# A decoder layer on one core: stacks of two heads by half of the tokens instead of one head by all of them, and keys as 1024 and chunks of 256

## The chip, the cores and the metric

The kernel runs on one core of a Trainium2 chip. Times are device microseconds (us) of that core, the median of several executions. A profile is one further execution. Its engines are called PE (TensorE), DVE (VectorE), ACT (ScalarE), POOL (GpSimd) and SP (the queue that issues most DMAs).

## What is computed

A post-norm decoder layer over 1024 tokens of width 128: self attention with 16 heads of width 8 that share one key and one value head, cross attention over 6404 context rows with a mask, and a top-1 mixture of 8 experts.

```
x = layernorm(x + attn(x))            # Q: 16 heads of 8; K = x@Wk+bk, V = x@Wv+bv: one head of 8 for all
x = layernorm(x + cross(x, ctx, mask))
    # scores = Q K^T / sqrt(8); where(mask == 0, -1e9, scores); softmax; @ V; @ Wo.T + bo
x = layernorm(x + ffn(x))
    # probs = softmax(x @ router_w.T + router_b); the expert of the largest one;
    # out = (x @ expert_w[e].T + expert_b[e]) * max(probs)
```

The mask of these inputs is the same for every token and leaves the last 1233 of the 6404 keys.

## The kernel before

*Units of work.* Both attentions run through the same pipeline. `Qs` holds, for each of 16 heads, a stack of two products: partitions 0 to 63 carry the queries of the first half of the tokens, partitions 64 to 127 those of the second half (`STACK`, index f). TensorE runs the two as one pair beside each other. Rows (queries on the output partitions, keys along the free dimension) are made only to find each query's maximum: VectorE reduces them (`mxs` L786, `mxc` L937). The maximum is split in two parts, turned by TensorE (`turn_max`, L1289), copied by ScalarE (`max_copy`) and stored by SP into rows of `Qs`, so that the column products (keys on the output partitions) come out with the maximum taken off. ScalarE makes the exponentials of the columns into `prob` (L1102, L1141), TensorE multiplies them by the values into bank O (`add_values`, L1319). `copy_o` takes O away, SP stores it to DRAM (`od`) and brings all heads back at the end (`o_back`).

*Steps.* A step is a column block of 128 keys for both halves, one row unit of a later head and the values of the block before. In self attention a head has 8 steps and 8 row units of 128 x 1024 (L1386 to L1416); rows are 15 units ahead. PSUM: two banks RT of 1024 columns for rows, three banks ST of 512 for columns, one bank O.

*Cross.* Keys are taken in pairs of blocks of PAIR = 640. A head has, for these inputs, n = 2 of them, so 10 steps. Its row units are RU = 6 for each 640 keys: four of 128 x 1024 (512 keys, two halves) and two that hold the last 128 keys of four tiles (128 x 512). `cross` (L1508) writes out the order by hand: `other_blocks`, `next_blocks`, `rows_pairwise`, with the banks of columns in the order BANK (L46). The keys of each head lie in DRAM (`kd`); SP loads them into a ring in `big` (`load_k`, L365) and POOL copies them rounded into `Kr` and `Kc` (`staged`, L544), values into `vst` (L572).

*What lies between the attentions.* After the last self values come: the sums back from DRAM, the reciprocal (L890), its spread over the heads (L1463), the projection (L1475), residual and norm (`statistics` L864, `normalised` L871), the turn of x (L1483), the cross queries (`project_q`), the keys and values of the second pair (L1448), and the loads of `Kl`. POOL counts the mask during self attention (L489 to L506); TensorE sums the counts at steps 117 and 118 (`count_live`), VectorE computes from them where the live keys begin (`steering`, L798), and every engine reads the result into a register.

*The end.* `finish` (L1660) projects, norms, turns x, makes the router logits and the products with all 8 experts (L1671), half of them weighed by VectorE (L995), half by ScalarE (L1180) with POOL's sums (L644).

Of the kernel before, what the change touches and what calls it, by code (L numbers as in the profile page):

```python
# [16 lines left out]
P = 128  # L17
# [7 lines left out]
PAIR = 640  # L25
NBLK = PAIR // P
NP = -(-KEYS // PAIR)
KPAD = NP * PAIR
FRONT = KPAD - KEYS
NB = KPAD // P  # L30

CW = PAIR // 2
CR = KPAD // CW
FLAG_AT = 384
MIN_PAIRS = 2
# [6 lines left out]
RU = 6  # L42
RS = NP + 2
NCOL = 2 * NBLK

BANK = (2, 0, 1, 2, 0, 1, 0, 2, 0, 1)  # L46
AGAIN = tuple(min(d for d in range(1, NCOL) if BANK[k - d] == BANK[k]) for k in range(NCOL))
SELF_U = 8
LA = 7
SLOTS = 5  # L50
HALFT = KPAD // 2
# [5 lines left out]
VW = DH + 1  # L57


def decoder_layer(nc, t, out):  # L60
    ctx = ExitStack()
    with ctx:
# [12 lines left out]

# [5 lines left out]
        bqrow = {a: sb(f"bqrow_{a}", [1, D]) for a in "sx"}  # L84
        bkrow = sb("bkrow", [1, DH])
        bv_x = sb("bv_x", [P, 1])
        krep = sb("krep", [P, 1])
        qrep = {a: sb(f"qrep_{a}", [P, DIRECT]) for a in "sx"}
        kcon = sb("kcon", [P, 1])
        qcon = sb("qcon", [P, DIRECT])  # L90
# [3 lines left out]
        bo = {a: sb(f"bo_{a}", [1, D]) for a in "sx"}  # L94
        wkr, bkr = sb("wkr", [P, 9, DH]), sb("bkr", [1, 9, DH])
        wq0 = {a: sb(f"wq0_{a}", [P, DIRECT, 9, DH]) for a in "sx"}
        bq0 = {a: sb(f"bq0_{a}", [1, DIRECT, 9, DH]) for a in "sx"}
        ident = sb("ident", [P, P])
        sel = sb("sel", [P, 8, HEADS, DH])
        penI = sb("penI", [P, P], BF16)  # L100
        ones = sb("ones", [P, P], BF16)
        onesf = sb("onesf", [P, P])
        orow = sb("orow", [1, P])
        zerof = sb("zerof", [P, (HEADS - DIRECT) * HALF * 4 // P])
# [4 lines left out]
        eps = sb("eps", [P, 1])  # L109
        Qs = sb("Qs", [P, HEADS, HALF], F32R)  # L110
        Kself = sb("Kself", [P, Q], F32R)
        Kc, Kr = sb("Kc", [P, NBLK, P], F32R), sb("Kr", [P, PAIR], F32R)
        vst = sb("vst", [P, NBLK, VW])
# [4 lines left out]
        ctxn = sb("ctxn", [P, 2, PAIR])  # L118
        kx_fa, kx_la, kx_ha = sb("kx_f", [P, PAIR]), sb("kx_lo", [P, PAIR]), sb("kx_hi", [P, PAIR], F32R)
        mxs = sb("mxs", [P, 2, 2, QT])  # L120
        mxc = sb("mxc", [P, 2, 2 * NP, QT])
# [5 lines left out]
        aTr = sb("aTr", [P, Q])  # L127
        den, rden = sb("den", [P, P]), sb("rden", [P, P])
        wcol = sb("wcol", [P, 2 * CR - 1], BF16)
        fl = sb("fl", [CR, 2])  # L130
        sm = sb("sm", [P, 2, NP])
        down = sb("down", [P, NP])
        steer = sb("steer", [1, 4], I32)
# [10 lines left out]


        KL_W, G_W = RS * PAIR, QT * PAIR // 2
        big = sb("big", [P, max(KL_W + 3 * G_W, 2 * HALFT + 3 * HALFT // 4 + KPAD // 2)], I32)
        maskI = [big[:, k * HALFT:(k + 1) * HALFT] for k in range(2)]
        m0 = 2 * HALFT
# [3 lines left out]
        Kl = big[:, 0:KL_W].bitcast(F32).rearrange("p (s k) -> p s k", k=PAIR)  # L153
        Qf = Qs[:, :, :].rearrange("p h q -> p (h q)")
        gint = big[:, KL_W:KL_W + G_W].rearrange("p (t k) -> p t k", k=PAIR)
        grow = big[:, KL_W + G_W:KL_W + 2 * G_W].bitcast(BF16).rearrange("p (t k) -> p t k", k=PAIR)
        gcol = big[:, KL_W + 2 * G_W:KL_W + 3 * G_W].bitcast(BF16).rearrange("p (t k) -> p t k", k=PAIR)
        we = big[:, 0:E * D].bitcast(F32).rearrange("p (e o) -> p e o", e=E)

        vroom = Vx[:, :, :, :].rearrange("p b h w -> p (b h w)")
        xroom = big[:, KL_W:KL_W + 3 * G_W].bitcast(F32)
        qfull = {a: r[:, 0:Q] for a, r in (("s", vroom), ("x", xroom))}
        qlow = {a: r[:, Q:2 * Q] for a, r in (("s", vroom), ("x", xroom))}
# [7 lines left out]
        fx = xT[0:CR, 3 * CW:3 * CW + 2 * CR]  # L173

        e_prod = vroom[:, 0:4 * Q].rearrange("p (t e) -> p t e", e=4 * D)
        e_two = vroom[:, 4 * Q:6 * Q].rearrange("p (t e) -> p t e", e=2 * D)
        e_sum = vroom[:, 6 * Q:7 * Q].rearrange("p (t e) -> p t e", e=D)
        aT, coefT = prob[:, 0, :], prob[0:E, 1, :]

# [1579 lines left out]
```

## Time and profile before

| | us |
|---|---|
| median of 3 runs | 506.13 (505.16 to 506.80) |
| span of the profiled execution | 505.4 |
| PE busy | 482.0 (95%) |
| DVE busy | 419.7 (83%) |
| ACT busy | 368.0 (73%) |
| POOL busy | 209.5 (41%) |

The time of the profiled execution by the clock of the runs isn't listed; its span is 0.7 under their median. Busy time is that in which an instruction of the engine was at work by the profile; for PE the ends are modelled, so that a full PE doesn't say that it couldn't be faster. "Idle before" is the time in which the engine stood before an instruction, with what released it. An engine's shares are means over stages with different limits, so the stages are read one by one. The mean granted clock of TensorE is 0.984 of full speed.

### The profile page before, as it was taken

Reading aid. Unit: us, or ns where it says so; the run is one execution under the profiler, and the core shown is the slowest. Engines: PE = TensorE matmul, PEld = TensorE weight load, DVE = VectorE, ACT = ScalarE, POOL = GpSimd, SP = SyncE. Lnnn points to the kernel's source line nnn. Section 1 sums busy time; section 2 is a strip of 40 time slices with the busy share of each in tenths; the row PEclk is TensorE's granted clock in tenths of the full one; section 3 lists DMA queues with packets and bytes.
Section 4 is the critical chain, followed back from the end, with each engine's and each line's share of the span. In section 5 each row is a group of like instructions: output and inputs, shape, how many; then the busy total and the mean of one; then the engine's idle time right before and its main releaser. Section 6 shows DMA issues by size and latency. Waiting matters only on the chain.

```text
span 505.4 us, 13819 instructions
## 1 busy us (share of the span) xinstructions
PE 482.0 (95%) x4122; PEld 197.3 (39%) x4122; DVE 419.7 (83%) x612; ACT 368.0 (73%) x718; POOL 209.5 (41%) x316
## 2 busy tenths in 40 slices
PE   7999999999999999987999999999999999999983
PEld 2433333333333344632344444444444444433641
DVE  5999999999999926668699989999899899831766
ACT  6358888888888875441678877877878887787263
POOL 4825755885469900132233323333233332320045
PEclk9899999999999999999799999999999999999997
DMA  4859864875453014524133110111111111010101
GB/s 116 350 147 305 280 219 166 298 259 194 167 173 137 12 54 123 161 62 121 42 71 81 41 40 26 40 37 30 38 32 40 40 40 40 27 40 22 43 1 45
DMA packets 21772, 52.58 MB, mean 104 GB/s; under 512 B 5021, under 2 KB 13375, under 8 KB 19649
## 3 DMA queue, kind: packets, MB, share of 16 engines
q1 hardware_dynamic: 18461, 22.46, 16.8%
q0 software_dynamic: 2304, 28.84, 15.4%
q8 instruction: 37, 0.61, 0.5%
q10 hardware_dynamic: 932, 0.37, 0.3%
q14 instruction: 38, 0.31, 0.2%
HBM read 42.10 MB, written 8.94 MB: 101 GB/s over the span
## 4 chain that ended last, share of the span: by engine, by line
PE 81%; DVE 9%; ACT 5%; issue 3%; DMA 1%; SPq 0%; DVEq 0%; POOL 0%; ACTq 0%; POOLq 0%
PE O L1321 32%; PE ST L1555 15%; PE RT L1527 10%; PE ST L1352 10%; PE RT L1338 5%; DVE mxs L786 3%; ACT prob L1102 2%; PE O L1292 1%; DVE mxc L937 1%; PE RT L1231 1%; ACT Vx L1180 1%; PE O L1317 1%; PE RT L1464 1%; ACT prob L1141 1%; PE RT L1679 1%
## 5 line engine op out<-in xcount | busy, mean ns | idle before, releaser
L937 DVE TENSOR_REDUCE mxc<-RT 128x1024 f32 (+1 forms) x192 | 196.1, 1045 | 23.4 <-PE RT L1527 18.9
L1141 ACT ACTIVATE prob<-ST 128x512 f32<-128x512 f32 x320 | 172.4, 596 | 38.7 <-PE ST L1555 36.8
L1102 ACT ACTIVATE prob<-ST 128x512 f32<-128x512 f32 x256 | 138.6, 597 | 24.7 <-PE ST L1352 14.1
L786 DVE TENSOR_REDUCE mxs<-RT 128x2 f32<-128x1024 f32 x128 | 152.7, 1224 | 2.8 <-PE RT L1338 0.6
L1527 PE MATMUL RT<-Kr,Qs 64*128 64x128 f32 (+1 forms) x512 | 121.8, 375 | 2.7 <-DVEq L924 1.2
L1555 PE MATMUL ST<-Qs,Kc 64*128 64x512 f32 x320 | 122.3, 458 | 2.0 <-DMA Qs<-qd_x 1.4
L1321 PE MATMUL O<-prob,vst 128*9 128x256 f32 x1280 | 100.3, 385 | 1.7 <-ACT prob L1141 1.3
L1338 PE MATMUL RT<-Kself,Qs 64*128 64x512 f32 x256 | 89.6, 454 | 1.8 <-DVE Kself L753 0.9
L1352 PE MATMUL ST<-Qs,Kself 64*128 64x512 f32 x256 | 91.2, 450 | 0.0
L1321 PE MATMUL O<-prob,Vs 128*9 128x256 f32 x1024 | 79.3, 381 | 1.5 <-ACT prob L1102 0.7
L1555 PEld LDWEIGHTS ST<-Qs,Kc 64*128 64x128 f32 x320 | 54.5, 187 | 61.2 <-issue 31.6
L1527 PEld LDWEIGHTS RT<-Kr,Qs 64*128 64x128 f32 x512 | 59.0, 186 | 23.8 <-DVE mxc L937 18.4
L572 POOL COPY vst<-Vx 128x27 f32 x64 | 13.1, 205 | 106.4 <-PE O L1321 105.5
L1352 PEld LDWEIGHTS ST<-Qs,Kself 64*128 64x128 f32 x256 | 37.4, 184 | 50.2 <-ACT prob L1102 37.5
L495 POOL TENSOR_SCALAR big<-big 128x3520 uint8<-128x3520 uint32 x16 | 50.0, 3127 | 7.2 <-DMA big<-in_mask 6.8
L547 POOL CAST Kr<-big 128x512 fp32r (+1 forms) x64 | 29.2, 456 | 39.4 <-PE RT L1527 21.1
L1321 PEld LDWEIGHTS O<-prob,vst 128*9 128x9 f32 x1280 | 19.0, 88 | 52.7 <-ACT prob L1141 42.7
L547 POOL CAST Kc<-big 128x256 fp32r (+1 forms) x64 | 29.2, 456 | 23.2 <-PE ST L1555 22.7
L1338 PEld LDWEIGHTS RT<-Kself,Qs 64*128 64x128 f32 x256 | 35.8, 185 | 7.5 <-DVE mxs L786 3.8
L1321 PEld LDWEIGHTS O<-prob,Vs 128*9 128x9 f32 x1024 | 15.2, 88 | 45.1 <-ACT prob L1102 38.5
L466 POOL DMA_DIRECT2D big<-in_mask x16 | 9.4, 588 | 49.1 <-DMA Qs<-mxr 35.4
L499 POOL TENSOR_TENSOR big<-big 128x880 int32<-128x880 int32 x14 | 29.1, 2080 | 1.2
(232 smaller groups left out, 355.4 us busy)
## 6 DMA issues: line engine op xcount, KB each, us to landing
big<-in_mask POOLq DMA_DIRECT2D x16, 1760.0 KB, 7.3
big<-kd SPq DMA_DIRECT2D x66, 80.0 KB
od_s<-osb SPq DMA_DIRECT2D x14, 128.0 KB, 1.9
od_x<-osb SPq DMA_DIRECT2D x14, 128.0 KB, 1.8
Qs<-qd_s SPq DMA_DIRECT2D x12, 128.0 KB, 6.3
Qs<-qd_x SPq DMA_DIRECT2D x12, 128.0 KB, 3.8
qd_s<-Vx SPq DMA_DIRECT2D x2, 512.0 KB, 4.8
qd_x<-big SPq DMA_DIRECT2D x2, 512.0 KB, 4.5
```

The costliest lines, as they stand in the source:

```text
L495: g_.tensor_scalar(sums if q == 0 else dead8, maskI[m % 2].bitcast(U32), 1.0, 0.0, ALU.min, ALU.max) \
L499: g_.tensor_tensor(sums.bitcast(I32), sums.bitcast(I32), dead8.bitcast(I32), ALU.add) \
L547: g_.tensor_copy(dst, Kl[:, ds(slot, 1), k0:k1].rearrange("p o k -> p (o k)")).then_inc(S(name), 1)
L786: v.tensor_reduce(mxs[:, h % 2, c2, :].rearrange("p (f t) -> p f t", f=2)[:, :, q], RT[r % 2][:, :].rearrange("p (f k) -> p f k", f=2), AX ...
L937: v.tensor_reduce(o, src, AX.X, ALU.max).then_inc(S("x_row_free"), 1)
L1102: nc.scalar.activation(prob[:, c % SLOTS, k * HALF:(k + 1) * HALF], ST[(2 * c + k) % 3][:, :], ACT.Exp) \
L1141: nc.scalar.activation(prob[:, b, (k % 2) * HALF:(k % 2 + 1) * HALF], ST[BANK[k]][:, :], ACT.Exp) \
L1321: mm = mmul(O[32 * q:32 * q + VW, 0:256], v, prob[:, slot, q * 256:(q + 1) * 256], start=False, stop=False, skip_group_check=True)
L1338: mm = mmul(RT[r % 2][:, f * HALF:(f + 1) * HALF], Qs[STACK[f], h, q * P:(q + 1) * P], Kself[STACK[f], c2 * 512:(c2 + 1) * 512], start=Tru ...
L1352: mmul(ST[(2 * c + f) % 3][:, :], Kself[STACK[f], b * P:(b + 1) * P], Qs[STACK[f], g, :], start=True, stop=True).then_inc(S("s_col_ready"), 1)
L1527: mm = mmul(o, Qs[STACK[f], h, q * P:(q + 1) * P], Kr[STACK[f], w], start=True, stop=not gen, skip_group_check=True)
L1555: mm = mmul(o[:, :], Kc[STACK[f], b, :], Qs[STACK[f], g, :], start=True, stop=not gen, skip_group_check=True)
```

## The change

A stack now holds two heads (f = 0 and 1) for one half of the tokens: unit j is the head pair j mod 8 of half j // 8 (`UNITS` = 16). So all heads of the first half are done after 8 units, in both attentions.

- *Order.* One list of steps covers both attentions: 128 of self, then 16 units of 10. Rows run LEAD = 15 units ahead across the border. Everything that belongs to a finished half is set between steps by number (`RT_JOBS`, `ST_JOBS`): for half 0 of self at steps 66 to 103 (projection, norm, x queries, the last 1024 keys and values, mask count, flags, steering), the further keys at step 104 (`KV`), half 1 of self in units 0 to 2 of cross, half 0 of cross in units 9 to 11, its expert products in units 14 and 15. The PSUM banks of rows and columns go round as rings in which such a job takes a turn.
- *Keys.* The last KS = 1024 keys are always used, then chunks of KC = 256; these inputs need one chunk. A unit has 10 row units of 128 x 1024: eight for 1024 keys, two with 256 keys of two tiles each.
- *Loads.* `Kr` and `Kc` are loaded directly from DRAM by DMAs of POOL (`load_rows`, `load_cols`: 10 a unit); `Kl`, `load_k` and `staged` are gone. SP keeps maxima, sums and queries.
- *Loops.* The usual case (one chunk, the same mask for all) is written out without loops on TensorE, POOL and ScalarE's main part; other masks take `any_keys` and `cross(True)`.
- *Norm.* The inverse root of three of the norms, and that of the first half's last norm, is made by POOL as a power of -0.5 instead of ScalarE's root. Output biases are added by POOL. Warm-up products between the attentions and before the end are gone.
- *Last half.* After the last step only half 1 of cross, its norm and experts, and the rest of half 0's experts are left (`finish`).

The core of the diff:

```diff
-PAIR = 640
-NBLK = PAIR // P
-NP = -(-KEYS // PAIR)
+KS, KC = 1024, 256
+SBLK, CBLK = KS // P, KC // P
+NBLK = SBLK + CBLK
-RU = 6
-BANK = (2, 0, 1, 2, 0, 1, 0, 2, 0, 1)
+UNITS = 16
+RU = 10
+LEAD = 15
...
+RT_JOBS = {74: ("s0 spread",), 77: ("s0 y",), 90: ("k",), 98: ("count",), 100: ("flags",), KV - 1: ("km",),
+           X(1, 0): ("s1 spread",), X(1, 4): ("s1 y",), X(9, 0): ("x0 spread",), X(9, 4): ("x0 y",),
+           X(10, 4): ("x0 logits",), X(14, 6): ("e0",), X(15, 1): ("e1",),
+           STEPS: ("x1 spread", "x1 y", "x1 logits", "e2", "e3")}
+ST_JOBS = {66: ("bias",), 85: ("s0 turn",), 88: ("s0 q",), 94: ("v0",), 96: ("v1",), KV: ("vm",),
+           X(2, 0): ("s1 turn",), X(2, 4): ("s1 q",), X(10, 2): ("x0 turn",), ...
...
+TURN = {**{SELF_U * g - 6: g for g in range(1, UNITS)}, SELF - 3: UNITS,
+        **{X(j, 7): UNITS + 1 + j for j in range(UNITS - 1)}}
...
+                for j in range(UNITS):
+                    if j:
+                        load_cols(j, 1)
+                        stage_v(j, 1)
+                    if j + 2 < UNITS:
+                        load_rows(j + 2, 1)
+                        load_rows(j + 2, 2)
+                    norm_work(j)
+                    if j + 1 < UNITS:
+                        load_cols(j + 1, 0)
+                        split_max(j + 1)
+                        stage_v(j + 1, 0)
+                    if j + 3 < UNITS:
+                        load_rows(j + 3, 0)
...
+                if h == 13:
+                    more_keys()
+                    sp.wait_ge(S("pen_made"), 1)
+                    for k, c in enumerate((*range(CHUNKS - 4, CHUNKS), CHUNKS - 5)):
+                        load(pd[:, k * KC:(k + 1) * KC], penr[32 * (c % 4) + c // 4:32 * (c % 4) + c // 4 + 1, :], "pen_out")
...
+            def row_products(o, U, u, f, gen):
+                if u < SRU:
+                    parts = [(u % 4, slice(512 * (u // 4), 512 * (u // 4) + 512), 0)]
+                else:
+                    parts = [(2 * (u - SRU) + k, slice(KS, KUSE), KC * k) for k in range(2)]
...
+            def add_values(v, slot):
+                for q in range(4):
+                    mm = mmul(O[32 * q:32 * q + VW, 0:256], v[q // 2], prob[:, slot, q * 256:(q + 1) * 256],
+                              start=False, stop=False, skip_group_check=True)
```

## Rows read from the trace of the kernel before

**Rows 1.** Busy by stage: stretch, length, each engine's busy us (instructions), PEclk, DMA, GB/s.

```profile
115.50:167.22 51.72, 51.42 (x500) 17.68 (x497) 50.65 (x60) 45.98 (x91) 33.80 (x15) 1.00 0.43 154
200.40:236.90 36.50, 32.20 (x168) 15.42 (x163) 27.64 (x54) 12.11 (x20) 8.08 (x14) 1.00 0.40 121
264.36:432.13 167.77, 167.50 (x1624) 71.58 (x1620) 152.57 (x157) 135.17 (x265) 56.54 (x168) 1.00 0.15 40
446.26:464.40 18.14, 16.11 (x148) 5.13 (x142) 0.47 (x1) 15.15 (x30) 3.01 (x10) 1.00 0.14 40
464.40:505.40 41.00, 31.33 (x146) 17.43 (x142) 28.46 (x111) 17.58 (x48) 12.06 (x13) 0.92 0.10 28
```

**Rows 2.** Timeline of VectorE in self attention: start, us, engine, line, operation, count.

```profile
115.50 9.59 DVE L786 TENSOR_REDUCE mxs<-RT 128x2 f32<-128x1024 f32 x8
...
125.84 2.36 DVE L786 TENSOR_REDUCE mxs<-RT 128x2 f32<-128x1024 f32 x2
```

**Rows 3.** Timeline of TensorE in self attention, a step's first column, and a head's end.

```profile
107.86 0.50 PE L1352 MATMUL ST<-Qs,Kself 64*128 64x512 f32 x1
...
112.72 0.49 PE L1352 MATMUL ST<-Qs,Kself 64*128 64x512 f32 x1
...
114.59 0.34 PE L1317 MATMUL O<-zrow 128*128 128x384 bf16 x1
...
115.46 0.39 PE L1292 MATMUL O<-ident,mxh 128*16 128x128 f32 x2
```

**Rows 4.** Timeline of VectorE over one head of cross attention.

```profile
334.27 0.48 DVE L947 TENSOR_REDUCE finx<-mxc 128x8 f32<-128x176 f32 x1
...
340.54 0.69 DVE L937 TENSOR_REDUCE mxc<-RT 128x512 f32 x1 [0.39 <-PE RT L1527]
...
348.26 0.48 DVE L947 TENSOR_REDUCE finx<-mxc 128x8 f32<-128x176 f32 x1
```

**Rows 5.** Groups by shape, 265 to 435: busy us, mean ns, idle before.

```profile
L1527 PE MATMUL RT<-Kr,Qs 64*128 64x128 f32 x192 | 26.5, 285 | 0.0
```

**Rows 6.** Groups by line, 160 to 237: busy us, mean ns, idle before.

```profile
L1369 PE MATMUL RT<-big,wcol 128*22 128x320 bf16 x22 | 3.3, 299 | 0.0
...
L876 DVE TENSOR_SCALAR x<-x,mv,rstd 128x128 f32<-128x128 f32 x8 | 2.2, 343 | 0.1
L1380 PE MATMUL RT<-ctxn,wk_x 128*128 128x512 f32 x4 | 2.2, 637 | 0.7 <-issue 0.7
...
L866 DVE BATCH_NORM_STATS2 stat<-x 128x6 f32<-128x128 f32 x8 | 1.7, 281 | 0.1
L1384 PE MATMUL RT<-wv_x,ctxn 128*128 128x128 f32 x10 | 1.5, 285 | 0.0
...
L890 DVE RECIPROCAL rden<-den 128x128 f32<-128x128 f32 x1 | 1.0, 952 | 0.9 <-DMA den<-osb 0.9
L844 DVE TENSOR_SCALAR kx_f<-RT,bk_x 128x640 f32<-128x640 f32 x1 | 0.9, 884 | 0.2 <-issue 0.2
```

**Rows 7.** Timeline where steering ends: its last write, and SP's load after it.

```profile
193.40 0.14 DVE L828 CAST steer<-sc 1x1 int32<-1x1 f32 x1
...
195.16 0.38 SPq L244 DMA_DIRECT2D ctxn<-in_ctxT  x1
```

**Rows 8.** Timeline of POOL: the mask counts are made ready for TensorE.

```profile
161.77 6.05 POOL L506 CAST big<-big 128x7040 bf16<-128x7040 uint8 x1
```

**Rows 9.** The ending: three pieces of the chain of work, one row of the timeline.

```profile
464.92 1.66 DMA den<-osb
...
484.77 1.14 ACT Vx L1180 x4
...
487.20 1.28 ACT L1205
...
498.35 1.27 POOL L671 TENSOR_TENSOR prob<-prob,Vx 128x512 f32<-128x512 f32 x1 [0.15 <-ACT prob L1190]
```

**Rows 10.** POOL's issues of the mask loads: ns min/median/max, first and last start.

```profile
L466 POOL DMA_DIRECT2D big<-in_mask x16: 541/576/743, 10.0 to 149.5; - x16
```

More of the change, by code:

```diff
@@ L291, in o_back @@
[L291 to L301 removed]
+            later = (UNITS - DIRECT) * HALF // P
@@ new lines, in _ @@
+            for h in range(2):
+                for k in range(2):
+                    sp.wait_ge(S(("q_high", "q_low")[k]), h + 1)
+                    load(qd["s"][k].rearrange("d h q -> h d q")[:, :, tokens(h)],
+                         (qhigh.bitcast(F32), qlow)[k][:, tokens(h)], "q_out")
+                if h == 0:
+                    sp.wait_ge(S("q_out"), 32)
+                    queries(DIRECT, 4, "q_in0")
+            max_rows(0)
+            queries(4, 8, "q_in")
+            for h in range(UNITS):
@@ L638, in _ @@
+            pool.wait_ge(S("kd_out"), 64)
+            pool.wait_ge(S("st_free"), number(ST_AT, "v1"))
+            before = steps[0]
+            with pool.If(slow == 0):
+                usual()
             with pool.Else():
-                stream(True)
-            step = 5
+                steps[0] = before
+                any_keys()
             def add(o, a, b):
-                g_.tensor_tensor(o, a, b, ALU.add).then_inc(S("pool_step"), 1)
-            def four_experts(q0, q1):
-                pool.wait_ge(S("y_part"), 4 * q1)
+                step(g_.tensor_tensor(o, a, b, ALU.add))
@@ new lines, in residual, with normalised @@
+            def residual(a, ph):
+                w = tiles(ph)
+                bank = ready(f"{a}{ph} y")
+                dve.wait_ge(S("x_bias"), 1 if a == "s" else 2 + ph)
+                freed(v.tensor_tensor(x[:, w, :], x[:, w, :], bank[:, 0:HALF].rearrange("p (t d) -> p t d", d=D), ALU.add))
+                dve.wait_ge(S("rt_free"), number(RT_AT, f"{a}{ph} y"))
+                statistics(ph, "var")
+            def normalised(o, ph, name):
+                for q in range(4 * ph, 4 * ph + 4):
@@ L951, in _, with norm @@
[L951 to L962 removed]
+            def norm(k, ph):
+                dve.wait_ge(S("std"), k)
+                normalised(x, ph, "xn")
@@ new lines, in _ @@
+            sums_back(4)
+            spread_rows("x", 1)
+            residual("x", 1)
+            dve.wait_ge(S("std"), 4)
+            ch(v.reciprocal(rstd[:, 4:8], rstd[:, 4:8]))
+            normalised(x, 1, "xn")
+            dve.wait_ge(S("bias_in"), 1)
+            statistics(0, "f_var")
+            router_max(1)
+            dve.wait_ge(S("f_std"), 1)
+            normalised(outs, 0, "out_done")
+            router_weights(1)
+            lower_experts(2)
+            lower_experts(3)
@@ L1722, in _ @@
+            with pe.If(slow == 0):
                 cross(False)
```

2224 lines of the change are left out of this document (1146 added, 1078 removed).

## The prediction

> **What bounds the kernel now.** I read the busy time by stage first, then each stage's pace on VectorE and TensorE, then the prices of the single steps, then the ends.
>
> The stages [rows 1] show five stretches. In five heads of self attention (115.50 to 167.22) VectorE is busy 50.65 of 51.72 us and TensorE 51.42. In twelve heads of cross attention (264.36 to 432.13) TensorE is busy 167.50 of 167.77, VectorE 152.57, ScalarE 135.17. Between the last self values and the first cross column (200.40 to 236.90) 36.5 us pass in which no exponential is made (ScalarE 12.11). The last 15 column steps have no rows beside them (446.26 to 464.40). After the last values come 41.0 us of ending.
>
> Self: the eight reductions of a head take 9.59 us (1.199 each) and the next head's begin 10.34 after this one's [rows 2]; the rest is the split of the maximum. TensorE's step is (112.72 - 107.86)/4 = 1.215 us, and at a head's end it also clears the output bank and turns the maximum [rows 3]: 10.34 - 8 x 1.215 = 0.62 more. Both engines are full at once: a step costs 1.2 us on either, and anything put between steps is paid.
>
> Cross: a head takes 348.26 - 334.27 = 13.99 us [rows 4]. VectorE needs 8 x 1.199 + 4 x 0.69 + 0.48, at most 12.8, and waits for TensorE (0.39 in the middle row, similar waits twice more per head). TensorE makes the last 128 keys of each 640 in pieces of 128 columns, 192 of them in that stretch with 285 ns each [rows 5]: 16 pieces a head with little work in each. So cross is held by small row products and by the fixed order around them, not by columns alone.
>
> **The change, part by part.** I follow the row stream, which sets the pace up to 15 steps before the end, and add what comes into it.
>
> *Up to the last self row.* Rows before, LEAD rows ahead, products and shapes are the same: 128 self rows, 8 per unit. The stream starts as now and the last self row would be reduced at 115.50 + 6 x 10.34 - 0.75 = 176.8 (six heads from [rows 2] on, without the last split) if nothing came between.
>
> *Work put between self steps* (half 0's projection and norm, its x queries, last 1024 keys and values, mask count, steering). VectorE can be one row behind, because RT has two banks. A job with p on TensorE and d on VectorE therefore costs max(1.2, p) + d - 1.2; a job on one engine alone costs itself. From [rows 6]: a 128-column fp32 product costs 0.15 a record (1.5 for 10), one of 512 columns 0.55 a record (2.2 for 4), two records each; VectorE takes 0.88 for 640 PSUM columns, so 0.7 for 512 and 1.3 for 1024.
> - spread: 0.7. Projection with residual and statistics: 0.7 + 0.9 + 0.3 = 1.9 (the 0.3: four small ones at the 0.14 of [rows 7], overlapped). Keys of 1024: p 2.2, d 2.6: 3.6. Mask count: 6656 columns at 3.3/7040: p 3.1, d 2.6 (four passes over 256 columns, six small ones): 4.5. Flags and steering: 2.1, ten ops at 0.2. Together 12.8.
> - TensorE alone: bias 0.3, turn 0.6, queries 1.1, values 2.3: 4.3.
> - VectorE alone: reciprocal 0.95, normalise 1.1 (four at 0.34, overlapped), small ones 0.5: 2.6.
>
> *Where the chunk is known* (step 104): TensorE, VectorE and ScalarE each read a register, and TensorE waits for the 256 keys that SP can only fetch then. Now SP's load is issued 1.76 us after steering's last write [rows 7]; with about 2 us to land it comes 4 us after, and steering ends 2 to 3 us ahead of step 104. Bounds: 1 (only the products, 1.2) and 8 (nothing overlaps); I take 4, near the middle, since both products and their two reductions (about 2) are certain. On SP the rows of maximum 14 stand behind the key stores, behind pd and its reload: 1 us. Behind TensorE's wait here stands everything.
>
> 176.8 + 12.8 + 4.3 + 2.6 + 4 + 1 = 201.5. The mask counting on POOL must be done by step 98 (about 168 now): it ends at 167.8 before [rows 8] under looser pacing (its last load waits for head 12; now for head 10, some 20 us earlier), so it is covered; without that cover TensorE would stand.
>
> *Steps 113 to 127*, self columns with cross rows: 15 x 1.215 + 2 x 0.5 = 19.2. The 36.5 us between the attentions are gone: what was in them is above. At 220.7 the first cross column.
>
> *Cross units.* 1280 keys as before (1233 are live, so one chunk of 256), but each unit has ten rows of 1024 columns and ten steps: no 128-column pieces; the banks go round in threes as in self. VectorE 10 x 1.199 + 0.48 = 12.5; TensorE 10 x 1.215 + 0.62 = 12.8. Bounds: 12.5 and 13.99. I take 12.8, because the step is now the self step. 14.5 units with rows: 185.6.
>
> *Norm work inside cross.* By the same prices, half 1 of self: 0.95 + 0.7 + 1.9 + 1.1 + 0.6 + 1.1 = 6.4. Half 0 of cross: the same without queries, plus logits and router (1.4 + 0.6): 7.3. VectorE's slack of 0.3 a unit pays back 1. On POOL the inverse root and the low queries stand in front of the next maximum in three units: 1 each. Sum 15.7; bounds 8 (VectorE and TensorE overlap fully) and 22.
>
> *Last 15 steps*: as now 18.14 minus the 0.6 of a turn: 17.5; two expert products of 2.2 each fall here, where VectorE is idle and ScalarE sets the pace (15.15 of 18.14): 1.5 each. 20.5.
>
> 220.7 + 185.6 + 15.7 + 20.5 = 442.5, where now 464.4 stands.
>
> *The ending*, half the tokens. The load back begins 0.5 after the last values and takes 1.7 [rows 9], reciprocal 1.0, spread 1.0, product 0.75, projection 1.2, residual to norm 3.5: 9.7. Turn, copy and logits 2.4: 12.1. VectorE then takes half 0's last statistics first (they wait for two POOL adds of 1.27 [rows 9] behind ScalarE's table load: 12.9 to 14.1), router maximum 1.5, outputs 1.1, weights 0.7: 17.4. ScalarE: four expert parts of 1.14, table load 1.3 [rows 9], copies and bias product 2.4: 25.7; POOL 1.3, VectorE 0.7 + 1.2, root and norm 1.7: 30.6; store 2. 32.6 against 41.0. Bounds 28 and 38.
>
> Span 442.5 + 32.6 = 475.1. The profiled execution has a span of 505.4, and the median of the runs is 506.13, 0.7 more: forecast **476 us**.
>
> *A rule against the change.* POOL's mask issues take 576 ns [rows 10], SP's load issue beside steering 380 [rows 7]. The Trainium skill, DMA: Bandwidth & Descriptors, section Issuing engine by pattern, wants simple loads on Sync and says that the software path is generally the slower; its Specifications give about 1 us to the first byte there against 0.6. The change moves the key loads from SP to POOL, ten a unit. By that rule each would land 0.4 later (an estimate from that page); they are issued five steps or more ahead, so it would add at most 0.4 at the first unit. The trace agrees on the issue; landing of such loads from POOL no row here shows. What remains of it, as a mechanism of rows, is the third rival.
>
> **The rivals.**
> 1. *Jobs overlap better* than one row: the 24 us put into self and cross cost 14. For: the engines' jobs are on different engines. Against: both are full in self [rows 2, 3]. 466 us.
> 2. *The cross unit stays slow*: its 13.99 comes from ScalarE's exponentials and the three ST banks, which stay, not from the small pieces. For: ScalarE is 80% busy and TensorE's queue reads as full [rows 1]. Against: self has the same columns and exponentials at 1.215. With 13.99, 14.5 x 1.2 = 17 more: 493 us.
> 3. *Slower*: POOL becomes late with the maximum. In each unit it issues two row loads after step 4 (6.1), two column loads, then splits (two small ops, 0.2 each, rounded up from the 0.14 of [rows 7]) and TensorE turns the maximum before step 7, at 8.8. With 0.58 an issue [rows 10] the split ends at 6.1 + 2.3 + 0.4 = 8.8: exactly then. At 1.1 us an issue it is 2.0 late, 15 times, 30 us: there the kernel is no faster; at 1.2 it gives 513. For: the margin is nil, and the loads are of another shape than the masks. Against: they have fewer rows than a mask load. At 0.8 an issue: 13 more, 489.
> 4. *The halves don't follow each other*: first cross keys, pd or queries come late at step 113 (SP stores, reloads, POOL loads after that, some 11 us in a window of 12). 10 us of standing: 486.
>
> **How the numbers follow.** Forecast 0.56 (468 to 486, with rival 4's smaller stalls in it); rival 1: 0.13; rival 2: 0.13; rival 3 at 0.8 an issue: 0.08, slower: 0.05; rival 4 in full: 0.05. About 0.3% is what a measurement of this kernel tells from no change. Faster 0.94, within 0.3% 0.01, slower 0.05. Range 464 to 496: it takes in rival 2 and the bounds of the unknown terms.
>
> **What would show it.** Right: cross reductions all of 1024, units of 12.8 apart; no stretch without exponentials before the first cross column at about 221; last values at about 442; an ending of 33. Wrong: units above 13.5 with idle of VectorE (rival 2), idle of TensorE before the turned maximum put down to POOL (3), a hole of over 6 us at step 104 or 113 (4), self units above 12 us between 120 and 175 (jobs dearer than priced), or TensorE at its lower clock after such a hole.

## The result, and the profile after

| | before | changed |
|---|---|---|
| median of the runs | 506.34 us (8 runs) | 510.18 us (8 runs, 507.7 to 514.9) |
| ratio | | 1.0078, 95% interval 1.0044 to 1.0113 |
| span of the profiled execution | 505.4 us | 510.2 us |

The changed kernel is slower by 0.8%: little, but the interval leaves out 1. I had forecast 476 us, faster with a chance of 0.94. The time is outside my range (464 to 496).

By stage first. The columns are those of [rows 1]: stretch, length, busy us of TensorE, its weight loads, VectorE, ScalarE and GpSimd (instructions), granted clock, DMA share, GB/s. The rows are five undisturbed heads of self attention, the self rows with jobs between them, the self columns beside cross rows, the cross units, the last 15 steps and the ending.

```profile
64.00:115.60 51.60, 51.31 (x497) 17.71 (x495) 50.53 (x61) 45.88 (x90) 45.43 (x29) 1.00 0.71 256
116.77:211.26 94.49, 79.53 (x677) 31.04 (x674) 77.97 (x113) 58.87 (x116) 37.08 (x29) 0.95 0.40 119
211.26:229.33 18.07, 18.02 (x183) 6.68 (x177) 17.32 (x16) 15.84 (x32) 4.37 (x10) 1.00 0.14 39
229.33:452.54 223.21, 205.53 (x1910) 81.91 (x1907) 190.30 (x201) 168.93 (x328) 86.69 (x202) 0.96 0.26 65
452.54:472.55 20.01, 19.44 (x157) 6.67 (x155) 4.32 (x16) 15.16 (x30) 1.87 (x6) 1.00 0.09 24
472.55:510.20 37.65, 22.13 (x80) 12.90 (x76) 16.09 (x68) 16.59 (x44) 13.41 (x15) 0.75 0.06 17
```

The first row is the pace of before. In the second, TensorE, which hardly rested in the self row of [rows 1], is idle for 15.0 of 94.5 us, and the clock is below 1. In the fourth it is idle for 17.7. The 36.5 us without exponentials of [rows 1] are gone, as the change meant. They came back as idle time inside the two attentions.

One cross unit without jobs, on VectorE, answers to [rows 4]:

```profile
321.97 0.54 DVE L952 TENSOR_REDUCE finx<-mxc 128x8 f32<-128x192 f32 x1
322.41 8.17 DVE L928 TENSOR_REDUCE mxc<-RT 128x2 f32<-128x1024 f32 x7
331.13 1.23 DVE L928 TENSOR_REDUCE mxc<-RT 128x2 f32<-128x1024 f32 x1 [0.55 <-PE RT L1687]
332.58 2.42 DVE L929 TENSOR_REDUCE mxc<-RT 128x1024 f32 x2 [0.23 <-PE RT L1687]
335.16 0.54 DVE L952 TENSOR_REDUCE finx<-mxc 128x8 f32<-128x192 f32 x1
```

It takes 13.19 us against 13.99 before, so the unit did become faster. Eight of the fifteen intervals between two of these `finx` rows are longer than that: 15.3, 20.2, 16.9, 19.3, 15.3, 19.4, 14.7 and 14.4 us.

What TensorE waited for between 40 and 472 (engine, tile, line, releaser: us in total, times, longest):

```profile
PE O L1433 <- POOL mxh L645: 8.2, 4, 2.5
PE ST L1558 <- DVE x L1037: 5.6, 1, 5.6
PE ST L1484 <- DMA Qs<-mxr: 5.1, 3, 2.7
PE ST L1694 <- DMA Kc<-kd: 4.0, 1, 4.0
```

These nine waits are 22.9 us. Seven of them, the holes, are placed one by one below; the other two are small (1.3 us at the last maximum, 0.4 for a row of maxima).

**Hole at 124.7, maximum 9.** The chain of work (start, us, what):

```profile
115.74 6.54 DMA od_s<-osb
122.34 0.60 SPq L315
...
125.53 2.03 DMA Qs<-mxr
127.61 0.49 PE ST L1484
```

Head 7's output store takes 6.54 us to land (median 1.9 before). SyncE waits for it, then issues the load back of half 0, five issues in 3.2 us. Only then does it issue the 8 KB of maximum rows for which TensorE stands.

**Hole at 148.6, normalise**, VectorE, GpSimd and TensorE in the timeline:

```profile
146.92 7.18 DVE L1037 TENSOR_SCALAR x<-x,mv,rstd 128x128 f32<-128x128 f32 x4
147.62 5.73 POOL L626 CAST big<-big 128x6656 bf16<-128x6656 uint8 x1
154.25 1.08 PE L1558 MATMUL ST<-ident,x 128*128 128x128 f32 x4 [5.61 <-DVE x L1037]
```

Four steps of 0.34 us take 7.18; one of them lasts 5.87, as long as GpSimd's conversion of the mask counts beside it.

**Hole at 179, maximum 12**, 2.0 us: its row was issued right behind four key stores of 512 KB each (landing in 5.5 us), and landed in 4.63 us. SyncE's issues:

```profile
171.15 4.41 SPq L315 DMA_DIRECT2D kd<-big  x4
175.60 1.26 SPq L315 DMA_DIRECT2D Qs<-mxr  x1
```

**Holes at 255.5, 275 and 381, the split of the maximum on GpSimd**, 2.5, 1.8 and 2.5 us. The chain of the first one:

```profile
254.36 0.29 DVE mv L1025 x4
...
255.06 0.65 POOL rstd L552
...
256.08 0.60 POOL Kc L681
...
257.47 0.21 POOL mxh L645
257.68 0.04 issue
257.72 0.39 PE O L1433 x2
```

The maximum itself was ready at 252.9, but GpSimd waited for the statistics first. At 275 it is the low part of the queries (0.46) and the sum of x and the bias (1.29) that stand in front of the split, with 0.8 us of standing between them.

**Hole at 302, column keys**, 4.0 us:

```profile
295.18 10.38 DMA Kc<-kd
305.60 0.79 PE ST L1694
```

This load, the second of a pair of 80 KB each, takes 10.4 us to land (median 2.1) beside the gather of half 1's queries, 1 MB in four transfers, issued at 292.8.

Behind most holes the granted clock is at its lower level (0.50, which is 1.2 GHz), first 2 us where TensorE works again behind the normalise hole, then 2 us in the first late unit:

```profile
156.00:158.00 2.00, 2.00 (x14) 0.63 (x12) 1.59 (x2) 1.09 (x2) 0.00 (x0) 0.50 0.02 4
260.00:262.00 2.00, 2.00 (x14) 0.63 (x12) 1.75 (x5) 1.03 (x2) 1.01 (x2) 0.50 0.10 27
```

Windows of 1 us show it there for 3 to 7 us after six of the seven holes; after the first one (124.7) it stays at 1.00.

### The profile page after: what moved, and what is told of

The parts are those of the page before. It is cut to its first block, busy times and chain, and to the rows that moved or that the text cites. A ratio compares the mean times of both kernels' runs of the same rounds, so it can differ in the third digit from the quotient of the medians.

```text
span 510.2 us, 10802 instructions
## 1 busy us (share of the span) xinstructions
PE 456.7 (90%) x3904; PEld 179.3 (35%) x3905; DVE 413.6 (81%) x564; ACT 362.9 (71%) x708; POOL 227.5 (45%) x331
## 4 chain that ended last, share of the span: by engine, by line
PE 62%; DVE 16%; DMA 6%; issue 5%; ACT 5%; POOL 3%; SPq 2%; ACTq 0%; POOLq 0%; DVEq 0%
PE O L1457 24%; PE ST L1694 11%; PE ST L1484 7%; PE RT L1687 6%; DVE mxs L912 5%; PE RT L1472 4%; DMA Qs<-mxr 3%; DVE mxc L928 3%; ACT prob L1252 3%; DMA Kc<-kd 2%; DVE x L1037 2%; PE RT L1581 2%; PE O L1433 1%; SPq L315 1%; DMA od_s<-osb 1%
## 5 line engine op out<-in xcount | busy, mean ns | idle before, releaser
L928 DVE TENSOR_REDUCE mxc<-RT 128x2 f32<-128x1024 f32 x128 | 151.6, 1224 | 25.5 <-PE RT L1687 25.1
L1687 PE MATMUL RT<-Kr,Qs 64*128 64x512 f32 (+1 forms) x384 | 117.2, 409 | 0.4 <-DVE mxc L928 0.2
L671 POOL DMA_DIRECT2D Kr<-kd x96 | 47.8, 502 | 123.3 <-PE RT L1687 107.5
L1484 PE MATMUL ST<-Qs,Kself 64*128 64x512 f32 x256 | 96.8, 452 | 5.2 <-DMA Qs<-mxr 5.1
L1694 PEld LDWEIGHTS ST<-Qs,Kc 64*128 64x128 f32 x320 | 51.9, 190 | 71.9 <-issue 38.3
L1687 PEld LDWEIGHTS RT<-Kr,Qs 64*128 64x128 f32 x384 | 53.1, 189 | 1.9 <-DVE mxc L928 1.0
L594 POOL TENSOR_SCALAR big<-big 128x3328 uint8<-128x3328 uint32 x16 | 47.4, 2965 | 9.7 <-DMA big<-in_mask 9.4
L929 DVE TENSOR_REDUCE mxc<-RT 128x1024 f32 x32 | 38.9, 1224 | 4.9 <-PE RT L1687 4.9
L681 POOL DMA_DIRECT2D Kc<-kd x64 | 31.9, 502 | 17.3 <-PE ST L1694 15.4
L598 POOL TENSOR_TENSOR big<-big 128x832 int32<-128x832 int32 x14 | 27.5, 1964 | 1.2
```

The source lines that it names most:

```text
L594: g_.tensor_scalar(sums if q == 0 else dead8, maskI[m % 2].bitcast(U32), 1.0, 0.0, ALU.min, ALU.max) \
L671: pool.dma_start(Kr[r:r + PROD, w].bitcast(F32), head_rows(U, f)[:, w]).then_inc(S(f"kr{part}"), 16)
L928: return v.tensor_reduce(o[:, :, u % 4], src, AX.X, ALU.max)
L929: return v.tensor_reduce(o[:, :, 2 * (u - SRU):2 * (u - SRU) + 2], src.rearrange("p f (t k) -> p f t k", t=2), AX.X, ALU.max)
L1484: st_done(mmul(st_place((c, f))[:, :], Kself[STACK[f], b * P:(b + 1) * P], Qs[STACK[f], g, :], start=True, stop=True))
L1687: mm = mmul(o_, Qs[STACK[f], U, q * P:(q + 1) * P], Kr[STACK[f], w], start=True, stop=not gen, skip_group_check=True)
```

## The experiments

The theory: the jobs cost about what I priced. The loss is small things that stand in a queue behind large ones (SyncE's issues, bytes in flight, GpSimd's order, VectorE beside GpSimd), each paid once as a hole and again at half clock. The rival: both engines are full, the jobs themselves cost the time, and a hole is only where the bill shows. Then removing a hole moves the time to the next step.

Every ratio below is to the kernel before, whose median moved between 506.0 and 507.1 us from one batch of runs to the next. The changed kernel's ratio is 1.0078 (1.0044 to 1.0113), and an experiment is told from it where the intervals don't overlap.

**1. Order of SyncE's issues.**

```
-  h == 8:  o_rows(7); o_back("s", 0, 8)        # maximum 9 comes behind
+  h == 8:  o_rows(7)
+  h == 9:  (behind max_rows(9)) o_back("s", 0, 8)
-  h == 11: key stores      h == 12: store and gather x queries
+  h == 12: key stores, store x queries      h == 13: gather, then more_keys()
+  pen_in loads behind max_rows(14)
```

> Same work; only the order of SyncE's issues is changed in self attention: maximum 9 goes ahead of the load back of half 0 (its reciprocal's row and four parts), maximum 12 ahead of the key stores, the gather of half 0's cross queries and the reload of the penalty rows one unit later, maximum 14 ahead of that reload. Theory (late rows): TensorE's holes at 124.7 (2.7 us) and 179 (2.0 us) come from a turned maximum that stands in SyncE's queue behind other issues, or behind their bytes, and the second one is followed by 4 us at half clock (2 us more). Expected: both holes gone, no fall of the granted clock between 170 and 190, 6 to 7 us less than the changed kernel's 510: 503.5, first cross column near 223. Rival (paid steps): VectorE and TensorE are both full there and the jobs between the steps set the time, a hole is only where the bill shows: the time goes to the next step, 509 to 510.

Measured: 510.58 us, ratio 1.008 (1.0047 to 1.0114). Nothing gained, though the waits for `Qs<-mxr` between 110 and 230 are gone. Two new holes took their place. On SyncE's queue the chunk's load now followed the gather, and the chain shows

```profile
190.43 4.15 DMA ctxm<-in_ctxT
194.58 0.04 issue
194.62 1.22 PE ST L1521 x4
```

where in the changed kernel it lands in 2.05. TensorE stood 2.9 us for it in place of 0.8, and the clock fell to its lower level for 7 us from 193.9. And GpSimd's mask work, which waits for maximum rows, also came earlier: a conversion now ran from 122.62 to 125.59 in place of 128.73 to 131.70, and VectorE met it with a copy of 22 columns, 0.18 us in the changed kernel:

```profile
123.85 1.79 DVE L1101 COPY downx<-down 128x22 f32<-128x22 f32 x1
```

Behind that, from 128.9, the clock was at its lower level for another 7 us. By its time this speaks for the rival; by its trace two holes were traded for two others. Experiments 9 and 10 come back to it.

**2. The split ahead of the norm work on GpSimd.**

```
-                    norm_work(j)
                     if j + 1 < UNITS:
                         load_cols(j + 1, 0); split_max(j + 1); stage_v(j + 1, 0)
+                    norm_work(j)
```

> Same work; on GpSimd the norm work of a unit (inverse root, low part of the queries, bias sum) goes behind the next column load, the split of the next maximum and the staging of values, in place of ahead of them. Theory (late maximum): TensorE's holes at 256, 275 and 381 (2.5, 1.8 and 2.5 us), all ahead of the turned maximum and put down to the split on GpSimd, go away, and with them 3 to 5 us each at half clock: the units of 20.24, 16.91 and 19.42 us become 15, 14.5 and 14.5: 12.5 us less, 497.5. Rival (paid steps): units stay within 1 us of 20, 17 and 19, since normalise, turn and statistics are what fill them: 509. In between: holes gone, but the root then comes late for normalise and gives 1 to 2 us a unit back: 502.

Measured: 499.32 us, ratio 0.9872 (0.9843 to 0.9901). Of the four waits for `POOL mxh`, 8.2 us, one of 1.3 is left. The three units take 17.39, 13.44 and 15.91 us in place of 20.24, 16.91 and 19.42, less by 9.8, half clock behind the holes included. On GpSimd the split now ends at 250.87 and the root starts at 252.13, ahead of what needs it:

```profile
250.67 0.20 POOL L645 TENSOR_TENSOR mxh<-finx,mxh 128x8 fp32r<-128x8 f32 x1
251.46 0.26 POOL L689 COPY vst<-Vx 128x90 f32<-128x90 f32 x1 [0.60 <-PE O L1457]
252.13 0.24 POOL L551 TENSOR_SCALAR rstd<-mv 128x4 f32<-128x4 f32 x1 [0.41 <-DVE mv L1025]
```

Moving this one line turns the change from a loss of 0.8% into a gain of 1.3%.

**3. The conversion of the counts after normalise.**

```
+            pool.wait_ge(S("xn"), 4)
             g_.tensor_copy(acc, acc8).then_inc(S("mask_counts"), 1)
```

> Same work; GpSimd makes the mask counts bf16 (5.73 us) only when the four normalise steps of half 0 are done. Theory (locked out): a normalise step takes 5.87 us in place of 0.34 because VectorE doesn't get to memory beside that conversion; with the conversion half a microsecond later the four take 1.1 to 1.4 us, TensorE's hole of 5.6 us at 148.6 goes away, and so do the 7 us at half clock behind it (3.5 us): 501.5, and the conversion itself ends near 154. Rival: normalise was long because one of its inputs came late (root or mean), so it is as long as before, 510. Second rival: lock out as said, but it now meets the next maximum's reductions in the same way and the time is the same, 509.

Measured: 503.6 us, ratio 0.9967 (0.9941 to 0.9994). Normalise takes 1.31 us and the conversion, 5.73 as before, runs beside five reductions that don't slow down (5.74 for five):

```profile
147.41 1.31 DVE L1038 TENSOR_SCALAR x<-x,mv,rstd 128x128 f32<-128x128 f32 x4
148.65 5.74 DVE L913 TENSOR_REDUCE mxs<-RT 128x2 f32<-128x1024 f32 x5
```

**4. Idle products in the ending.** 2 and 3 around the spread, 6 ahead of the turn, 3 ahead of the logits, in bank O.

> Fourteen idle products of 512 bf16 columns are put into TensorE's ending, where it stands waiting anyway: 2 and 3 around the spread, 6 ahead of the turn, 3 ahead of the logits. Theory (clock): the ending is 37.7 us in place of 32.6 because TensorE falls to half clock from 478 on: fp32 products of 512 columns take 0.95 a record instead of 0.47. With the clock held the ending is 33.5 to 34.5 us: 506. Rival: ScalarE's expert parts and VectorE's and GpSimd's sums set the ending, TensorE's clock costs nothing on the path: 510, though the granted clock is near 1.

Measured: 507.8 us, ratio 1.0032 (1.0008 to 1.0056). This interval overlaps the changed kernel's, so the gain rests on the traces. The ending takes 34.52 us in place of 37.65, its mean clock is 0.89 in place of 0.75:

```profile
471.18:505.70 34.52, 20.97 (x93) 11.19 (x90) 16.59 (x68) 16.17 (x44) 13.39 (x15) 0.89 0.07 18
```

**5. The clock alone, one hole.** `warm_up(o, 26)` ahead of the wait for half 0's turn.

> The changed kernel with 26 idle products of 512 bf16 columns in TensorE's queue ahead of the turn of half 0 in self attention, in the bank that the turn then overwrites; nothing else is touched, and normalise is as slow as before, so that TensorE can't go on any earlier. It measures what the granted clock costs by itself. Theory (each long hole is paid twice, once as standing and once as half clock behind it): the turn starts at 154 as before, the clock then is 1.00 in place of 0.50 for the next 7 us, the steps there are 1.2 us in place of 2.1: 3.0 to 3.5 us less, 507. Rival: the steps behind the hole are slow for another reason (ScalarE or banks catching up): 510.

Measured: 510.48 us, ratio 1.0063 (1.004 to 1.0086): not told from the changed kernel. Its trace shows the clock held,

```profile
156.00:158.00 2.00, 2.00 (x24) 0.61 (x21) 2.00 (x3) 1.86 (x4) 0.00 (x0) 1.00 0.01 4
```

with 24 matmul records in the 2 us that held 14. From the start of normalise to the first step on the keys pass 18.8 us in place of 21.6, of which 0.5 is a shorter normalise: 2.3 us for the clock, less than the 3.0 to 3.5 expected. (The idle products held TensorE some 0.4 us beyond normalise and took that back.)

**6. Half 1's gather in four portions** (units 8 and 9 in unit 3, then two units more in each of units 4 to 6).

```
-                    gather_x_queries(1)          # 1 MB at once, in unit 3
+                if 3 <= j < 7:
+                    gather_two(j - 3)            # 0.25 MB
```

> Same work; the gather of half 1's cross queries (1 MB in four transfers, 292 to 306) is cut into four portions of two units each, one in each of units 3 to 6. Theory (bytes in front): the 4.0 us that TensorE stands at 302 for the second half of a unit's column keys, which were issued at 294.7 and landed 10.4 us later, are gone, and with them 7 us at half clock: the unit of 19.3 us becomes 13.5; 5.5 to 6 us less, 504.5. Rival: the transfers are slow because of their shape (16 partitions, 2 KB rows), wherever they stand: each of the four portions then delays a unit by about 1 us, 508 to 510.

Measured: 504.83 us, ratio 0.9967 (0.9935 to 0.9999). The wait for column keys is gone, loads of keys between 280 and 330 land in 2.0 to 2.3 us in the median (up to 3.1), and the unit of 19.27 takes 13.19. The portions have the shape of the whole, so it was not the shape but the bytes in flight at once.

**7. Another form of normalise.**

```
-                    v.tensor_scalar(o[:, q, :], x[:, q, :], mv[:, q, 0:1], rstd[:, q:q + 1], subtract, mult)
+                    v.scalar_tensor_tensor(out=o[:, q, :], in0=x[:, q, :], scalar=mv[:, q, 0:1],
+                                           in1=rstd[:, q:q + 1].to_broadcast([P, D]), op0=subtract, op1=mult)
```

> Same work; normalise is written with two operands from memory (tile and a broadcast column) in place of one tile and two columns of scalars; GpSimd's conversion starts where it did in the changed kernel, before the last three of the four. Theory: it is the one-tile form of VectorE that is kept out of memory while GpSimd converts; the two-operand form is not: four steps in 1.1 to 1.4 us, no hole at 148.6, about the time of the kernel with the later conversion (503.6). Rival: any VectorE operation from memory stands until GpSimd is done: 7 us for the four again, 510.

Measured: 511.38 us, ratio 1.0111 (1.0072 to 1.015): the rival's answer. The two-operand form stands just as long:

```profile
146.15 7.16 DVE L1037 SCALAR_TENSOR_TENSOR x<-x,mv,rstd 128x128 f32<-128x128 f32 x4
```

So my account of which form is kept out was wrong, and what did help was to start GpSimd's conversion later (experiment 3). What did run undisturbed beside GpSimd's mask operations: every reduction, and the reciprocal (0.94 us at 130.39, conversion from 128.73 to 131.70).

**8. All together** (the combination): the orders of 1, 2 and 3, the ending of 4, and the gathers of both halves in portions, only the first ahead of the chunk's load. Normalise and two small VectorE steps (the copy of 22 columns and the scaling of a bias) are in the two-operand form of 7 as well.

> All together: maximum rows first in SyncE's order, the gathers of both halves in portions of two units (the first alone ahead of the chunk's load), the split ahead of the norm work on GpSimd, the conversion after normalise, normalise and three small VectorE steps in the two-operand form, 14 idle products in the ending. Theory (holes add up, each with its half clock): less by 11 (split), 6.5 (conversion), 2.5 (ending), 5.5 (gather of half 1) and 4 to 6 (maxima 9 and 12, chunk's load no longer behind the gather of half 0): 510 - 30 = 480, between 476 and 486; no fall of the clock between 60 and 440. Rival (paid steps): what the holes hid is work that must be done anyway, and the gains overlap: 488 to 492, with VectorE idle little less than now.

Measured: 480.47 us, ratio 0.9498 (0.9454 to 0.9542). By stage (steps with jobs left out: first the self columns beside cross rows, then the cross units, the last 15 steps, the ending), and what TensorE still waits for most between 40 and 443:

```profile
197.81:216.30 18.49, 18.43 (x185) 6.97 (x179) 17.75 (x16) 16.23 (x32) 4.36 (x10) 1.00 0.20 55
216.30:423.20 206.90, 199.16 (x1906) 80.47 (x1903) 189.12 (x201) 168.23 (x327) 86.49 (x202) 1.00 0.27 72
423.20:443.30 20.10, 19.51 (x158) 6.68 (x156) 4.36 (x17) 15.19 (x30) 1.86 (x6) 1.00 0.08 24
443.30:478.40 35.10, 21.69 (x93) 11.88 (x90) 16.73 (x68) 16.17 (x44) 13.39 (x15) 0.86 0.06 18
```

```profile
PE O L1471 <- ACT prob L1266: 3.0, 13, 0.2
PE RT L1486 <- DVE mxs L924: 1.5, 1, 1.5
PE O L1447 <- POOL mxh L657: 1.3, 1, 1.3
```

No maximum row and no key load is late any more. The rival's 488 to 492 is outside the interval. One hole of the new order is left, and the forecast that the clock would not fall between 60 and 440 missed it: the copy of 22 columns again met a mask conversion (122.53 to 125.50), now in the two-operand form, TensorE stood 1.5 us for the reduction behind it, and the clock was at its lower level for some 3.5 us from 127.

```profile
123.28 2.27 DVE L1113 TENSOR_TENSOR downx<-down,onesf 128x22 f32<-128x22 f32 x1
```

**9. SyncE's order and portions without the rest.**

> SyncE's order of the first experiment (maxima 9, 12 and 14 ahead of other issues), and the gathers of the cross queries of both halves in portions of two units, of which only the first (0.25 MB) stands ahead of the chunk's load. GpSimd, VectorE, ScalarE and the ending as in the changed kernel. The first experiment gave nothing although both holes were gone: its chunk's load took 5 us to land behind 1 MB of gathered queries, and a copy of 22 columns on VectorE took 1.8 us beside a mask conversion. Theory: with the portions the chunk's load lands in 2 us as before and the order is worth 3 us (maximum 12 and part of 9), and half 1's portions are worth 5.5: 501 to 502. Rival: the order is worth nothing, since something else comes late each time: 504.5, the time of the gather's portions alone.

Measured: 502.56 us, ratio 0.9934 (0.9907 to 0.9962). The chunk's load lands in 2.02 us again, in place of experiment 1's 4.15 (the 5 of the expectation is too high). The copy of 22 columns takes 2.36 us beside a mask conversion here, but no fall of the clock follows. The centre is near the theory's, but the intervals of this and of experiment 6 overlap, so what the order gives by itself isn't settled here.

**10. All but SyncE's order and half 0's portions** (and without the two-operand forms).

> The combination without the change of SyncE's order and without portions for half 0: split ahead of norm work, conversion after normalise, portions for half 1, idle products in the ending. What it lacks against the combination (480.5) is what the order is worth in company. Theory: holes of 2.7 and 2.0 us for maxima 9 and 12 are back, the second with 4 us at half clock: 484.5 to 485.5. Rival (order worthless, as it was alone): 480.5 to 481.5.

Measured: 488.46 us, ratio 0.964 (0.9595 to 0.9684). Against experiment 8 that is 1.4%, 7 us, where 4 to 5 was expected. The hole for maximum 9 is 3.2 us here. Unlike in the changed kernel, the clock falls behind it, and VectorE waits at once:

```profile
128.59 1.23 DVE L922 TENSOR_REDUCE mxs<-RT 128x2 f32<-128x1024 f32 x1 [3.50 <-PE RT L1482]
```

The first cross row is reduced at 203.89 in place of 197.81. That is 6.1 us for the order in company, net of what the copy costs in the combination. From there to the last maximum both kernels take the same (224.8 and 224.9 us). The rest of the difference between the two traces, 3.7 us, is the ending, which fell to half clock at 460 here in spite of the same idle products (the traced execution took 489.8 us).

**11. A further step.** The copy of 22 columns and the bias scale go to GpSimd; in the ending, half 1's router ahead of half 0's last statistics, the last table load behind the bias copies, and 12 more idle products. Normalise is back in its old form.

> The combination, with the penalty countdown's copy and the bias scale moved from VectorE to GpSimd (in the combination that copy of 22 columns took 2.27 us beside a mask conversion, and TensorE fell to half clock for 5 us behind it), and with the ending changed: half 1's router maximum and weights ahead of half 0's last statistics on VectorE, the last table load behind the two bias copies on ScalarE, 12 idle products ahead of the last bias product. Expected: 2 to 2.5 less for the copy, 3.0 for the expert parts that start at 459 in place of 462 after the same beginning, 1.3 for the table load, 0.8 for the product at full clock; 7 in all if nothing else comes last, 473.5. If the ending is held by half 0's outputs or GpSimd's sums, 476.5 to 477.

Measured: 477.43 us, ratio 0.9434 (0.9404 to 0.9463), the fastest; 5.7% faster than before. The copy's 2.3 us are there: from head 8's first reduction to the reciprocal 10.8 us pass in place of 13.1, seven reductions in a row without a pause:

```profile
119.16 8.50 DVE L927 TENSOR_REDUCE mxs<-RT 128x2 f32<-128x1024 f32 x7 [0.36 <-PE RT L1482]
```

The ending gave little: from the last `finx` to the end 55.0 us in place of 55.7, where 5 less was expected. The clock was at half from 454 to 458. The idle products themselves took 2.42 us for six there (1.47 in the combination) and stood ahead of the turn, and the upper experts' products stood behind the lower ones, so that the parts on ScalarE began at 461.5, not 459. The traced execution took 479.7 us at a mean clock of 0.982, the other three 476.5 to 477.6 at 0.989 to 0.992, so this fall of the clock need not be in them.

**12. The clock alone, five holes**, each filled by idle products.

> The changed kernel with idle products in front of five of its holes, each in a bank that the next product overwrites: 26 ahead of half 0's turn, 11 ahead of the turned maximum of units 1, 2 and 9 (steps 7), 18 ahead of the column step that waits for late keys (unit 4, step 5). No wait and no transfer is changed, so every hole is as long as before; only the clock behind them can differ. It prices the clock alone more surely than the single filling did (2.3 us by its trace, not resolved by its times). Theory (a hole costs its length and then half clock for some 4 to 7 us): 2.3 + 3 x 1.8 + 3 = 10 to 11 us less, 499.5. Rival (the clock costs nothing beyond the hole, since VectorE is a row behind and holds the steps): 508 to 510.

Measured: 505.89 us, ratio 0.999 (0.9966 to 1.0014), between theory and rival: 4.5 us less than the changed kernel. From 230 to 460 the mean clock is 1.00 in place of 0.96:

```profile
230.00:460.00 230.00, 221.53 (x2044) 88.96 (x2040) 192.01 (x215) 176.62 (x344) 88.27 (x208) 1.00 0.25 65
```

The last maximum is ready at 445.33 in place of 452.04. 6.7 us less for some 25 us at half clock (0.04 x 2 x 223 = 18 in cross, and 7 behind normalise) is 0.27 us for each of them; by the medians, 4.5 us less, it is 0.18. I had expected about 0.4. The idle products at 275 ended 0.6 us after the maximum was ready, so the clock alone is worth a little more than this shows. My reading, which no run tests: VectorE is a row behind TensorE when a hole ends and catches up while TensorE runs slowly.

## Why the prediction was wrong

Where my clock of the kernel stood, the changed kernel, and the combination of experiment 8 (us from the start):

| | predicted | changed | combination |
|---|---|---|---|
| last self row reduced | 201.5 | 210.4 | 197.0 |
| first cross column | 220.7 | 229.3 | 215.9 |
| last row maximum | 422.0 | 452.5 | 423.2 |
| last values | 442.5 | 472.6 | 443.3 |
| span | 475.1 | 510.2 | 478.4 |

*What held.* The self rows without jobs, the 15 steps between (18.1 for 19.2) and the last 15 (20.0 for 20.5) are as priced. The 36.5 us between the attentions went. The prices of the jobs stand in the combination. There the long units (the last, of 13.55, with them) cost 14.4 above 13.19, where I had 15.7, and the self jobs 20.2, where I had 24.7. Its span is 3.3 us over the forecast, and part of that nearness is luck: self jobs dear by 4.5 stand against cross units cheap by 6.0 and an ending cheap by 2.5. The rival of paid steps is refuted by this: with the same work, 30 us went.

*What failed, first: every wait between the jobs.* The prediction priced each job on TensorE and VectorE and took what feeds them as ready; the seven holes, 21 us of standing, were in its sum with 4 at most (1 for maximum 14, 1 for each of three units). The right kind of step is in it twice, both times too small or in the wrong place. "On SP the rows of maximum 14 stand behind the key stores": it was maxima 9 and 12, behind the load back and the key stores. And the store ahead of that load back took 6.5 us beside the mask loads. Next, "On POOL the inverse root and the low queries stand in front of the next maximum in three units: 1 each": the three holes were 2.5, 1.8 and 2.5, and experiment 2 shows 9.8 us for the three units. The root costs more than its own 1.3 us. It costs also the wait for the statistics (1.9 us at 255.5), which come with the residual two steps before the turn; GpSimd stands through it with a finished maximum in hand. I listed what was queued and didn't ask when the first of the queue could start.

*Second: VectorE beside GpSimd.* "VectorE alone: ... normalise 1.1" was 7.18. In the kernel before, GpSimd's conversion of the counts [rows 8] ran beside reductions only, so no row showed it. The move put normalise beside it. The Trainium skill, SBUF — State Buffer, section Who interferes with whom, says that a VectorE operation in a two-port mode, or one with two inputs from SBUF against a GpSimd operation that reads SBUF, and the GpSimd operation exclude each other for whole instructions, that copies and tensor_scalar can be in such a mode, and that tensor_reduce on this chip never is. The trace agrees in each case here: normalise in both forms (7.18 and 7.16), the copy (1.79), reductions undisturbed. The prediction weighed a rule on transfers, and not this one, which was against the change.

*Third: the clock.* The list of signs names it, but the sum had no term for it. [rows 1] show 1.00 in four of five stretches. The changed kernel makes holes, and the rows at 156 and 260 show what follows. It costs 4.5 us by the times and 6.7 by the profile (experiment 12), besides 3.1 in the ending. There the kernel before kept TensorE busy with 28 idle products between 464.8 and 475.9, most of them in these two groups:

```profile
464.80 2.76 PE L1231 MATMUL ST<-wrow 128*128 128x512 bf16 x12
471.57 3.19 PE L1231 MATMUL ST<-wrow 128*128 128x512 bf16 x14
```

[rows 1] shows 0.92 for its ending; the change leaves them out and has 0.75. I had read those products as work that could go. The Trainium skill, TensorE: Matmul & The Clock Gate, section HAM oscillation — how this bites in real kernels, describes such falls where waits separate the products. The rows agree for six of the seven holes (0.50 behind them) and not for the first, of 2.7 us, where the clock stays at 1.00.

*Fourth: transfers.* The gather of half 1's queries had no cost in my sum ("the same without queries"), and held the column keys 4.0 us: 6 us for that unit (19.27 against 13.19, experiment 6). The rule I did weigh (GpSimd's loads land later) changed nothing. An issue takes 0.50 us (0.58 was taken), a load lands in 2.1, and in quiet units nothing waits for it, so rival 3 was right that GpSimd would be late with the maximum, and wrong on why.

*The size of a term:* a quiet unit is 13.19, where I had 12.8. I took turn and clear together at 0.62 from the end of a self head. In cross they are in different steps, 0.48 and 0.57, together 1.05. That makes 5.6 us over 14.5 units, and it is in the combination too. Rival 1 (jobs 10 us cheaper) does not describe the changed kernel, but the combination shows 5.8 of its 10; its "24 us put into self and cross" is the self part of the sum alone, with cross it is 40.4. Rival 2 is right by a third of its size (0.4 of its 1.2 a unit) and not by its cause: the turn and the clear are on TensorE, and TensorE waits for an exponential about once a unit, 0.2 us each time. Rival 4, keys or queries late at step 113, didn't happen: TensorE is busy 18.02 of the 18.07 us from 211.26. At step 104, where the sum has 4, TensorE waits 0.8 for the chunk's load.

The account: 35.1 us over the sum. 8.6 are there at the first cross column: 12.2 over the combination (holes for maximum 9, normalise and maximum 12, with the clock), 1.2 a later start, less 4.8 that I had overpriced. 14.7 are in long units, 5.6 in the 13.19 of every unit, 1.7 in the first and last pieces of units, and 5.0 in the ending; the last 15 steps give 0.5 back.

Open stays why one hole of 2.7 us is followed by no fall of the clock and one of 1.8 is; the same hole for maximum 9 is followed by a fall in experiments 2 and 10. Open stays also how surely idle products hold the clock in the ending: with the same fourteen it fell at 460 in one kernel and at 468 in another.

## What to carry to other kernels

When work is moved between the steps of a full pipeline, price its steps on the two full engines, but find its holes on the others: for each queue (SyncE, GpSimd, the bytes in flight) write down what stands ahead of the one small thing that the full engine waits for, and when the first of those can start. The maximum's row of 8 KB goes ahead of stores and loads back, the split of a ready maximum ahead of work that still waits for its input, a megabyte is cut into portions. And look at what VectorE will run beside each long GpSimd operation.

## What the runs showed of the hardware

- A copy of 22 columns (0.18 us alone) took 1.79 and 2.36 us beside a mask conversion on GpSimd in two kernels and, written with two operands, 2.27 in a third: the length of a VectorE operation says nothing of what it can lose there.
- Half clock costs less than the half of each us that its ratio suggests: 0.27 us by the traces and 0.18 by the medians (experiment 12), in a pipeline where VectorE is nearly as full as TensorE.
- A load of 80 KB took 10.4 us to land behind 1 MB in flight, and one of 128 KB took 4.15 in place of 2.05 behind another gather. With the gathers in portions both kinds landed in some 2 us.
